# An own order for the last three tiles of a two-layer attention block, with biases added by TensorE there

## The chip, the cores and the metric

The kernel runs on one core of a Trainium2 chip. A core has five engines with queues of their own: PE (TensorE, matrix products into the eight banks of PSUM; PEld is its loading of the stationary operand), DVE (VectorE), ACT (ScalarE), POOL (GpSimd) and SP (SyncE, which here only issues DMAs). Each engine takes its instructions strictly in the order in which the program lists them, and waits at semaphores for the others. The metric is the device time of one execution in microseconds (us), lower is better.

## The reference

2048 tokens (32 sequences of 64) of width 256 pass through a mixture of experts, an attention of 16 heads of 64 with tanh projections, an attention of 16 heads of 16 with a modulated softmax, and a linear layer on values rounded to four bits:

```
moe:   gate = softmax(rms(x) @ wg + cond @ gg); the top two experts of eight, three dense layers each
attn:  q, k, v, out = tanh(... @ W + b);  p = softmax(causal(q k' / 8));  x1 = x + tanh((p v) Wo + bo)
cond2: q, k, v = x1 @ Wqkv' + b;  p = softmax(q k' / 4)
       c   = sigmoid(tanh([x1, cond] @ Wc1' + bc1) @ Wc2' + bc2)          # per token and head
       p   = p * c / (c + 1e-8) scaled by (1 - FI), plus FI * field[key]  # FI = 0.21
       a   = (p v) @ Wout' + bout
ffn:   out = x1 + mxfp4(a) @ mxfp4(W)' + bffn       # blocks of 32 share a power-of-two scale
```

The lines on cond2 are cut down to what is computed for each token; `field` is one vector of 64 shares for each sequence.

## The kernel before

The expert stage runs first (the first 320 us). Then the two attention layers run over TT = 16 tiles of 128 tokens, that is two sequences each. All buffers of that stage lie in `arena`; `ps` is the whole of PSUM.

The order on each engine is written out by hand. PE's loop (`for t in range(2, TT + 4)` at the end of the PE block) mixes four stages of four tiles in one iteration: layer one of tile t (`l1_q`, `l1_k`, `l1_v`, `l1_scores`), its second half for tile t-1 (`l1_turn_p`, `l1_context`, `l1_out`), layer two of tile t-2 (`l1_turn_x1`, `l2_hidden`, `l2_q_or_k`, `l2_coherence`, `l2_scores`, `l2_v`) and of tile t-3 (`l2_turn_p`, `l2_context`, `l2_out`, `l2_turn_q`), and the last product of tile t-4 (`l2_ffn`). ACT's and DVE's loops follow the same pattern. From t = 16 on there is no layer one of a new tile: helpers drop out where their tile does not exist (`exists`), and what is left runs in the same order. PE then executes `tail_busy`: 190 products of constants into an unused bank, whose results nobody reads.

The steps of layer two of one tile, in the order in which one needs the other:

- `l1_out` (L931) on PE, `l1_bias_o` (L1799) on DVE, tanh on ACT (L1281), `l1_residual` (L1808) on DVE gives x1.
- PE turns x1 (L939), ACT copies it into `x1_t` (L1287). From it PE makes the hidden part (L962), q and k (both L947) and v (L981). ACT finishes hidden (L1315), q (L1294) and k (L1304).
- PE computes the coherence (L971) and the scores (L994). DVE takes their maximum (L1844, two halves) and subtracts it (L1850, two halves), ACT takes the exponential (L1330, two halves), DVE sums (L1864) and scales by `r2` (L1865 to L1867, L1872, result `p2`).
- PE turns p2 (L897, two halves), DVE copies it with the field share added (L1881, into `pt2`), PE makes the context (L1015), ACT copies it (L1336), PE makes `a` (L1024), DVE adds the bias (L1888, into `a_rows`).
- DVE rounds to four bits: `block_scales` (L1401 to L1409) and `round_blocks` (L1413 to L1421). PE turns the result (L1032), ACT copies (L1342), PE multiplies (L1041), DVE adds up the output (L1908, `fin`), SP stores it.

Each of these buffers exists once. `l2_x1_bias` (L1816) keeps x1 plus the last bias, and has to wait until L1908 of the tile before has read its buffer; the second half of `l2_turn_p` waits for L1908 of the tile before, since it writes the same bank. A step through `Steps` waits until the instruction before it on DVE is complete.

## Time and profile before

| | us |
|---|---|
| median of 3 runs | 757.79 |
| lowest, highest | 756.41, 757.93 |
| the profiled execution | 760.11 |
| its span, first to last instruction | 758.0 |

In the profiled execution PE is busy for 717.5 us of the span, PEld for 617.0, DVE for 504.8, ACT for 283.2, POOL for 87.4. The whole attention stage lies between about 320 us and the end. A row of a timeline gives the start and the duration of an instruction (or of a run of equal ones), then engine, line and operation; the duration holds the delay until the result is there, and the next instruction can start before it is over.

### The profile page before, as it was taken

The page shows a single profiled execution, that of the slowest core. Times are in us where ns is not written, and L with a number is a line of the kernel's source. Part 1 is how long each engine was busy: PE and PEld are TensorE (multiplying, and loading weights), DVE is VectorE, ACT ScalarE, POOL GpSimd, SP SyncE. Part 2 cuts the span into 40 slices and gives each one's busy share as a digit, 9 for nine tenths or more (in the row PEclk, how much of TensorE's full clock was granted, in tenths as well). Part 3 has the DMA queues.
Part 4 walks back from the last instruction along what each step waited for, and adds up shares of the span by engine and source line. Part 5 has one row for each costly group of instructions (what it writes and reads, how often), then busy time and mean ns, then how long its engine had stood idle before and what let it go on. Part 6 is the DMA issues. An engine that isn't in the chain of part 4 may idle for free.

```text
span 758.0 us, 20462 instructions
## 1 busy us (share of the span) xinstructions
PE 717.5 (95%) x8252; PEld 617.0 (81%) x8252; DVE 504.8 (67%) x1096; ACT 283.2 (37%) x827; POOL 87.4 (12%) x93
## 2 busy tenths in 40 slices
PE   6389999999999999999999999999999999999885
PEld 2279999569999999968888987897888888888774
DVE  3846564744443544244787888789778878887975
ACT  3032221141212112245445545544564555445421
POOL 2131112411212100121101110111011001000000
PEclk9599999999999999999999999999999999999999
DMA  7798111217101103210000010110011000000000
GB/s 285 296 354 313 37 36 58 81 45 257 41 32 43 36 22 112 84 36 22 22 11 22 29 31 2 29 29 23 9 30 30 16 16 29 16 9 9 16 9 15
DMA packets 21257, 49.13 MB, mean 65 GB/s; under 512 B 3179, under 2 KB 14827, under 8 KB 18605
## 3 DMA queue, kind: packets, MB, share of 16 engines
q1 hardware_dynamic: 12112, 32.47, 11.9%
q0 software_dynamic: 3744, 10.49, 4.6%
q10 hardware_dynamic: 5309, 4.87, 1.9%
q8 instruction: 66, 1.08, 0.6%
q14 instruction: 26, 0.21, 0.1%
HBM read 41.00 MB, written 6.82 MB: 63 GB/s over the span
## 4 chain that ended last, share of the span: by engine, by line
PE 87%; DVE 6%; another core or an unknown queue 3%; DMA 1%; ACT 1%; issue 1%; DVEq 0%; SPq 0%; POOL 0%; ACTq 0%; POOLq 0%
PE ps L745 15%; PE ps L846 15%; PE ps L715 8%; PE ps L872 7%; PE ps L779 7%; PE ps L931 7%; PE ps L947 3%; PE ps L897 3%; PE ps L890 2%; PE ps L922 2%; PE ps L1024 2%; PE ps L962 2%; PE ps L981 2%; PE ps L739 1%; PE ps L1041 1%
## 5 line engine op out<-in xcount | busy, mean ns | idle before, releaser
L846 PE MATMUL ps<-arena,l_weights 128*128 128x128 f32 x1024 | 125.9, 277 | 0.5 <-ACT arena L1241 0.5
L745 PE MATMUL ps<-h_t,w_now 128*128 128x128 f32 x1056 | 123.4, 275 | 1.2 <-DVE h_t L1623 1.2
L745 PEld LDWEIGHTS ps<-h_t,w_now 128*128 128x128 f32 x1056 | 120.5, 192 | 1.5 <-issue 1.5
L846 PEld LDWEIGHTS ps<-arena,l_weights 128*128 128x128 f32 x1024 | 119.3, 192 | 2.3 <-ACT arena L1241 1.0
L1166 ACT ACTIVATE h_t<-ps,cols 128x128 f32<-128x128 f32 x132 | 37.6, 367 | 164.1 <-PE ps L715 149.2
L1598 DVE COPY w_now<-arena 128x2048 f32 x33 | 40.5, 1227 | 83.9 <-PE ps L745 76.6
L1247 ACT ACTIVATE arena<-ps,cols 128x128 f32<-128x128 f32 x256 | 74.0, 388 | 46.6 <-PE ps L846 46.6
L610 POOL DMA_INDIRECT arena<-expert_out,slot_of x32 | 33.0, 1032 | 325.5 <-DVE arena L1651 278.6
L715 PEld LDWEIGHTS ps<-xg_t,w_now 128*128 128x128 f32 x528 | 63.4, 192 | 6.6 <-ACT xg_t L1149 4.1
L715 PE MATMUL ps<-xg_t,w_now 128*128 128x128 f32 x528 | 65.0, 276 | 3.6 <-ACT xg_t L1149 3.6
L579 POOL DMA_INDIRECT xg<-in_x,slot_tok x36 | 41.4, 1151 | 188.4 <-PE ps L694 156.4
L779 PE MATMUL ps<-arena,h_t 128*128 x264 | 62.4, 379 | 0.0
L872 PE MATMUL ps<-l_weights,arena 128*64 128x512 f32 x256 | 61.8, 604 | 0.0
L931 PE MATMUL ps<-l_weights,arena 128*128 128x256 f32 x256 | 58.9, 383 | 0.0
L931 PEld LDWEIGHTS ps<-l_weights,arena 128*128 128x128 f32 x256 | 47.4, 190 | 6.0
L779 PEld LDWEIGHTS ps<-arena,h_t 128*128 128x128 f32 x264 | 47.6, 190 | 5.1
L1582 DVE COPY w_now<-arena 128x1024 f32 x33 | 22.9, 694 | 29.3 <-PE ps L715 15.6
L897 PE MATMUL ps<-ident,arena 128*128 128x128 f32 x256 | 38.5, 273 | 1.4 <-DVE arena L1872 1.1
L1623 DVE TENSOR_SCALAR h_t<-ps,cols 128x128 f32<-128x128 f32 x128 | 35.8, 342 | 4.6 <-PE ps L745 4.5
L1767 DVE TENSOR_TENSOR arena<-ps,half_rows 128x512 f32<-128x512 f32 x32 | 21.9, 685 | 24.1 <-PE ps L922 18.6
L872 PEld LDWEIGHTS ps<-l_weights,arena 128*64 128x64 f32 x256 | 15.6, 136 | 22.5 <-issue 21.4
L947 PE MATMUL ps<-arena 128*128 128x128 f32 x256 | 33.7, 275 | 0.0
(303 smaller groups left out, 1077.5 us busy)
## 6 DMA issues: line engine op xcount, KB each, us to landing
arena<-in_experts SPq DMA_DIRECT2D x16, 1024.0 KB, 7.2
expert_out<-y ACTq DMA_DIRECT2D x36, 128.0 KB
arena<-in_x_t SPq DMA_DIRECT2D x2, 1024.0 KB, 6.0
arena<-in_x SPq DMA_DIRECT2D x16, 128.0 KB
out<-arena SPq DMA_DIRECT2D x16, 128.0 KB, 1.7
b<-in_b SPq DMA_DIRECT2D x1, 1024.0 KB, 7.2
l_weights<-in_wq SPq DMA_DIRECT2D x1, 1024.0 KB
l_weights<-in_wk SPq DMA_DIRECT2D x1, 1024.0 KB
```

The costliest lines, as they stand in the source:

```text
L579: pool.indirect_dma_start(out=xg[j % XG][:, :], out_offset=None, in_=t_in["x"], in_offset=bass.IndirectOffsetOnAxis(ap=slot_tok[:, slot_ti ...
L715: last = mm(ps[:, 0, m * P:(m + 1) * P], w1_now[:, k, m * P:(m + 1) * P], xg_t[:, k, :], start=k == 0, stop=k == KH - 1)
L745: last = mm(ps[:, 2, m * P:(m + 1) * P], w2_now[:, k, m * P:(m + 1) * P], h1_t[j % 2][:, k, :], start=k == 0, stop=k == KM - 1)
L779: last = mm(bank(4, HID), h2_t[j % 2][:, k, :], flat[:, bass.ds(at + k * HID, HID)], start=k == 0, stop=k == KM - 1)
L846: last = mm(ps[:, b, c * P:(c + 1) * P], wt[:, k, f:f + P], m_t[:, k, :], start=k == 0, stop=k == KH - 1)
L872: last = mm(ps[r * SEQ:(r + 1) * SEQ, value_bank(t, s), :], m_t[:, k, s * SEQ:(s + 1) * SEQ], wv[:, k, r * 512:(r + 1) * 512], start=k == ...
L897: last = pe.transpose(bank_[:, m * P:(m + 1) * P], p[:, h:h + 2, :], ident[:, :])
L931: last = mm(bank(1, HID), ctx_t[:, c, :], wo[:, c, :], start=c == 0, stop=c == C1 - 1)
L947: last = mm(ps[:, b, c * P:(c + 1) * P], wt[:, k, c * P:(c + 1) * P], x1_t[:, k, :], start=k == 0, stop=k == KH - 1)
L1166: last = f(h1_t[j % 2][:, k, :], ps[:, 0, k * P:(k + 1) * P], ACT.Relu, bias=cols[:, bass.ds(e * KM + at + k, 1)])
L1247: last = f(dst[:, cc, :], ps[:, project_bank(t, n), c * P:(c + 1) * P], ACT.Tanh, bias=col(bias)[:, cc:cc + 1])
L1598: dve.tensor_copy(w2_now[:, :, :].rearrange("p k n -> p (k n)"), arena[:, bass.ds(at, KM * MID)]).then_inc(w2_set, 1)
```

## The change

1. The loops end at t = 15 (PE, ACT) and with `first_part(TT)` (DVE). What is left of tiles p = 13, q = 14, r = 15 is written out as a list on each engine, with PSUM banks chosen by hand (`T1_END` to `FFN_END`). Work of three tiles is mixed there.
2. Layer two has two sets of buffers, chosen by `t % 2`, in the place where the experts' third weights lay. The output has two buffers and two semaphores (`stored`).
3. In these lists PE adds four biases as one more product with a matrix that has ones in its first row only (`first_row`, `first_of_half`), and the field share as a second product with the same stationary operand. DVE or ACT then reads PSUM directly: there is no L1799, no L1888, no L1822, and ACT copies `pt2` and v. POOL adds `x1_bias` for these tiles. Halves of p and of the sums are handed on apart.
4. Layer two in all tiles: `coh` is one operation in place of two, `l2_sums` has one operation less, and the scale by 0.25 in `block_scales` is folded into `act_inv` (two operations more in side stage 8 of the experts).
5. `tail_busy` is gone (190 products); `end_busy(30)` stands before the last tile's last two steps.

```diff
@@ PE
-            def tail_busy(t, last, n): ...
+            def end_out1(t):
+                if t == TT - 1:
+                    pe.wait_ge(pt2_set, 2 * (t - 2) + 1)
+                pe.wait_ge(ctx_set, 2 * t + 2)
+                dst = bank(O_END[t], HID)
+                mm(dst, first_row, row("bo"), start=True, stop=False)
+                for c in range(C1):
+                    last = mm(dst, ctx_t[:, c, :], wo[:, c, :], start=False, stop=c == C1 - 1)
+                last.then_inc(o_ps, 1)
...
+            def end_context2(t):
+                pe.wait_ge(pt2_set, 2 * t + 2)
+                pe.wait_ge(v2_set, 2 * t + 2)
...
+                            mm(dst, values, pt2[t % 2][:, 2 * g + r, q], start=True, stop=False, tile_position=(0, g * PAIR))
+                            last = mm(dst, values, field_t[:, t, q], start=False, stop=True, tile_position=(0, g * PAIR))
+                last.then_inc(out2_ps, 1)
...
-            for t in range(2, TT + 4):
+            for t in range(2, TT):
...
-                tail_busy(t, TT + 2, 20)
...
-                tail_busy(t, TT, 14)
-                tail_busy(t, TT + 1, 20)
...
-                tail_busy(t, TT, 12)
...
-                tail_busy(t, TT, 10)
-                tail_busy(t, TT + 1, 44)
...
-                tail_busy(t, TT + 2, 70)
                 l2_turn_q(t - 3)
-                l1_out(t - 1)
+                if t < TT - 1:
+                    l1_out(t - 1)
+
+            p, q, r = TT - 3, TT - 2, TT - 1
+            pe.wait_ge(first_row_set, 5)
+            end_out1(q)
+            l2_ffn(p - 1)
+            end_turn_p1(r, 0)
+            end_turn_x1(q)
+            end_turn_p1(r, 1)
+            end_q2(q)
+            end_k2(q)
+            end_turn_p2(p, 0)
+            end_context1(r)
+            end_scores2(q)
+            end_turn_p2(p, 1)
+            end_out1(r)
+            end_context2(p)
+            end_turn_x1(r)
+            end_out2(p)
...
+            end_turn_p2(r, 0)
+            end_turn_p2(r, 1)
+            end_ffn(p)
+            end_context2(r)
+            end_out2(r)
+            end_turn_q(q)
+            end_ffn(q)
+            end_busy(30)
+            end_turn_q(r)
+            end_ffn(r)
@@ DVE
             def l2_coherence(t):
...
-                step(ts(coh, ez, 1.0, None, ALU.add))
-                step(dve.reciprocal(coh, coh))
+                step(ts(coh, ez[t % 2], MOD_EPS / (1.0 - FI), (1.0 + MOD_EPS) / (1.0 - FI), ALU.mult, ALU.add))
+
+            def l2_divide():
+                step(tt(r2, coh, z2, ALU.mult))
+                step(dve.reciprocal(r2, r2))
...
+            def end_scales(t):
+                dve.wait_ge(a_ps, t + 1)
+                block_scales(step, bank(OUT2_END[t], HID), q_amax, q_scale, q_inv, None)
+
+            def end_round(t):
+                round_blocks(step, bank(OUT2_END[t], HID), xq[t % 2], q_tmp, q_mag, q_scale, q_inv, act_inv[:, 1:2]).then_inc(xq_set, 1)
...
+            p, q, r = TT - 3, TT - 2, TT - 1
+            first_part(TT)
...
+            end_sum2(q, 0)
+            l1_residual(r)
+            end_sum2(q, 1)
+            end_scales(p)
+            end_round(p)
+            l2_coherence(q)
+            l2_divide()
+            end_share2(q, 0)
+            end_share2(q, 1)
+            l2_max(r, 0)
+            l2_shift(r, 0)
+            l2_max(r, 1)
+            l2_shift(r, 1)
+            l2_coherence(r)
+            end_sum2(r, 0)
+            end_sum2(r, 1)
+            l2_divide()
+            end_share2(r, 0)
+            end_share2(r, 1)
+            end_scales(q)
+            end_round(q)
+            end_result(p)
+            end_scales(r)
+            end_round(r)
+            end_result(q)
+            end_result(r)
@@ POOL
+                if t == 1:
+                    pool.memset(v2[1], 0.0).then_inc(v2_zeroed, 1)
+                    pool.memset(first_row, 0.0).then_inc(first_row_set, 1)
...
+            for t in range(TT - 3, TT):
+                pool.wait_ge(x1_set, t + 1)
+                pool.wait_ge(fin_set, t - 1)
+                pool.wait_ge(x1_bias_set, t)
+                pool.tensor_tensor(x1_bias[t % 2], x1, row("bffn"), ALU.add).then_inc(x1_bias_set, 1)
```

PE in the middle of the end, before: the coherence and `a` of one tile, q and k and the scores of the next, with constant products (L1048) wherever the next step is not ready.

```order
L971 MATMUL ps<-cols,arena 128x16 x2
L1024 MATMUL ps<-arena 128x256 x2
L947 MATMUL ps<-arena 128x128 x8
L1048 MATMUL ps<-before 128x128 x20
L994 MATMUL ps<-arena 64x128 x16
L1048 MATMUL ps<-before 128x128 x44
L981 MATMUL ps<-arena 64x128 x8
L1032 MATMUL ps<-before,arena 128x128 x2
```

The same place now: L1124 turns x1 of tile 15, L1213 is the bias product and L1215 the product with Wout of tile 13, L1149 hidden and L1130 q and k, L1156 and L1159 coherence, L1166 and L1170 v, L1186 the scores of tile 15, and L942 turns p2 of tile 14.

```order
L1124 MATMUL ps<-ident,arena 128x128 x2
L1213 MATMUL ps<-rows,arena 128x256
L1215 MATMUL ps<-arena 128x256 x2
L1149 MATMUL ps<-arena 128x128 x4
L1130 MATMUL ps<-arena 128x128 x8
L1156 MATMUL ps<-rows,arena 128x16
L1159 MATMUL ps<-cols,arena 128x16 x2
```

Real products of another tile stand where the constant ones stood.

DVE in the same stretch, before: the output bias of layer one, the result of one tile, x1 of the next, the two halves with the field share, and then the wait for `a` (L1888) before anything else.

```order
L1799 TENSOR_TENSOR arena<-ps,rows 128x256
L1908 SCALAR_TENSOR_TENSOR arena<-ps,act_inv,arena 128x256
L1816 TENSOR_TENSOR arena<-arena,rows 128x256
L1808 TENSOR_TENSOR arena<-arena 128x256
L1881 TENSOR_TENSOR arena<-ps,arena 128x512 x2
L1888 TENSOR_TENSOR arena<-ps,rows 128x256
L1822 TENSOR_TENSOR arena<-ps,rows 128x16
L1401 TENSOR_REDUCE arena<-arena 128x8
```

DVE now, from the end of the rounding of tile 13 (L1741): coherence (L2179), the divisor (L2182, L2183), the two halves of p2 of tile 14 (L2257), then maximum and shift of tile 15 by halves, its coherence and its sums (L2253).

```order
L1741 TENSOR_TENSOR arena<-arena 128x256
L2179 TENSOR_SCALAR arena<-arena 128x16
L2182 TENSOR_TENSOR arena<-arena 128x16
L2183 RECIPROCAL arena<-arena 128x16
L2257 TENSOR_TENSOR arena<-arena 128x512 x2
L2166 TENSOR_REDUCE arena<-ps 128x8
L2172 TENSOR_TENSOR arena<-ps,arena 128x512
L2166 TENSOR_REDUCE arena<-ps 128x8
L2172 TENSOR_TENSOR arena<-ps,arena 128x512
L2179 TENSOR_SCALAR arena<-arena 128x16
L2253 TENSOR_REDUCE arena<-arena 128x8 x2
```

The operations on x1, on the field share and on the biases have left this stretch, and the next tile's scores follow directly on the p2 of the one before.

## Rows read from the trace of the kernel before

**Rows 1.** The page's first part: busy us, share and instructions of each engine.

```profile
PE 717.5 (95%) x8252; PEld 617.0 (81%) x8252; DVE 504.8 (67%) x1096; ACT 283.2 (37%) x827; POOL 87.4 (12%) x93
```

**Rows 2.** Busy time by stretch: PE, PEld, DVE, ACT, POOL, granted clock, DMA share, GB/s.

```profile
24.00:28.00 4.00, 0.00 (x0) 0.00 (x0) 3.69 (x23) 0.00 (x0) 0.00 (x0) 0.50 0.86 297
...
550.00:600.00 50.00, 50.00 (x721) 42.20 (x719) 40.66 (x87) 26.74 (x78) 4.19 (x4) 1.00 0.08 23
...
708.00:712.00 4.00, 3.11 (x48) 2.75 (x49) 3.90 (x6) 1.56 (x6) 0.00 (x0) 1.00 0.14 39
...
744.00:748.00 4.00, 1.84 (x41) 1.34 (x41) 2.65 (x5) 0.37 (x1) 0.00 (x0) 1.00 0.10 33
```

**Rows 3.** DVE's timeline from 680 us: outputs of five tiles, one wait.

```profile
680.25 0.48 DVE L1908 SCALAR_TENSOR_TENSOR arena<-ps,act_inv,arena 128x256 f32<-128x256 f32 x1 [0.20 <-PE ps L1041]
...
689.68 0.42 DVE L1888 TENSOR_TENSOR arena<-ps,rows 128x256 f32<-128x256 f32 x1 [3.27 <-PE ps L1024]
...
705.93 0.48 DVE L1908 SCALAR_TENSOR_TENSOR arena<-ps,act_inv,arena 128x256 f32<-128x256 f32 x1
...
725.67 0.48 DVE L1908 SCALAR_TENSOR_TENSOR arena<-ps,act_inv,arena 128x256 f32<-128x256 f32 x1
...
744.58 0.48 DVE L1908 SCALAR_TENSOR_TENSOR arena<-ps,act_inv,arena 128x256 f32<-128x256 f32 x1
...
755.45 0.48 DVE L1908 SCALAR_TENSOR_TENSOR arena<-ps,act_inv,arena 128x256 f32<-128x256 f32 x1 [1.68 <-PE ps L1041]
```

**Rows 4.** The chain that ended last: start us, us, what ran.

```profile
701.73 3.51 PE ps L931 x16
...
707.08 0.44 DVE arena L1808
...
709.65 0.94 ACT arena L1315 x4
...
738.47 0.70 DVE arena L1850
...
746.84 0.70 PE ps L1015 x32
747.56 0.38 ACT arena L1336
747.95 0.04 issue
747.99 1.15 PE ps L1024 x4
...
753.83 0.30 PE ps L1032 x2
...
754.58 0.84 PE ps L1041 x6
```

**Rows 5.** DVE's timeline: one tile's rounding, first, a small and last operation.

```profile
749.62 0.42 DVE L1401 TENSOR_REDUCE arena<-arena 128x8 f32<-128x256 f32 x1
...
750.48 0.17 DVE L1406 TENSOR_SCALAR arena<-arena 128x8 f32<-128x8 f32 x1
...
753.35 0.43 DVE L1421 TENSOR_TENSOR arena<-arena 128x256 bf16<-128x256 f32 x1
```

**Rows 6.** ACT's timeline: tanh, four parts of k, two copies of p.

```profile
705.98 0.42 ACT L1281 ACTIVATE arena<-arena 128x256 f32<-128x256 f32 x1 [3.04 <-DVE arena L1799]
...
714.47 1.50 ACT L1304 ACTIVATE arena<-ps,cols 128x128 f32<-128x128 f32 x4 [0.60 <-PE ps L947]
...
716.80 1.08 ACT L1275 COPY arena<-ps 128x512 f32<-128x512 f32 x2
```

**Rows 7.** The one memory fill by POOL at 306 us: duration in ns.

```profile
L615 POOL MEMSET arena<- x1: 524/524/524, 305.9 to 305.9; 128x512 f32 x1
```

**Rows 8.** PE's timeline: turning p, constant products.

```profile
744.60 1.17 PE L897 MATMUL ps<-ident,arena 128*128 128x128 f32 x8 [1.07 <-DVE arena L1872]
...
748.96 4.07 PE L1048 MATMUL ps<-before 128*128 128x128 bf16 x70
```

More of the change, by code:

```diff
@@ L1050, in _, with end_ffn @@
+            def end_ffn(t):
+                pe.wait_ge(xqt_set, t + 1)
+                dst = bank(FFN_END[t], HID)
+                for k in range(KH):
+                    for n in range(PARTS):
+                        last = mm(dst, xq_t[t % 2][:, k, :], wffn[:, k, n, :], start=k + n == 0,
+                                  stop=(k, n) == (KH - 1, PARTS - 1))
+                last.then_inc(f_ps, 1)
             layer1(LAST)
@@ new lines, in end_tanh_o, with end_x1t, end_q2 @@
+            def end_tanh_o(t):
+                act.wait_ge(o_ps, t + 1)
+                act.wait_ge(x1_set, t)
+                f(o_rows, bank(O_END[t], HID), ACT.Tanh).then_inc(o_set, 1)
+            def end_x1t(t):
+                act.wait_ge(x1t_ps, t + 1)
+                act.copy(x1_t[t % 2], bank(X1_END[t], HID).rearrange("p (k q) -> p k q", k=KH)).then_inc(x1t_set, 1)
+            def end_q2(t):
+                act.wait_ge(qk2_ps, 2 * t + 1)
+                for c in range(C2):
+                    last = f(q2_t[t % 2][:, c, :], ps[:, Q2_END[t], c * P:(c + 1) * P], ACT.Identity,
+                             bias=col("bq2")[:, c:c + 1])
+                last.then_inc(qk2_set, 1)
@@ new lines, in end_ez, with end_v2 @@
+            def end_ez(t):
+                act.wait_ge(z_ps, t + 1)
+                f(ez[t % 2], bank(Z_END[t], H2), ACT.Exp, scale=-1.0).then_inc(ez_set, 1)
+            def end_v2(t):
+                act.wait_ge(v2_ps, t + 1)
+                for odd in range(2):
+                    part_ = slice(odd * SEQ, (odd + 1) * SEQ)
+                    act.copy(v2[t % 2][part_, :, odd * D2:(odd + 1) * D2],
+                             ps[part_, V2_END[t], 0:HID].rearrange("p (m d) -> p m d", d=D2)).then_inc(v2_set, 1)
@@ L1366, in _ @@
             l1_exp(1, 1)
-            for t in range(2, TT + 3):
+            for t in range(2, TT):
                 l1_m(t)
@@ L1924, in _, with first_part @@
             l1_residual(0)
-            for t in range(3, TT + 4):
+            def first_part(t):
                 l1_mix(t)
@@ L1944, in _ @@
                 l1_ctx(t - 2, 1)
+            for t in range(3, TT):
+                first_part(t)
                 l2_sums(t - 3)
```

367 lines of the change are left out of this document (310 added, 57 removed).

## The prediction

> **What bounds the kernel now.** I read the busy table first, then the stretches, then DVE's timeline and the chain of waits near the end. PE is busy for 717.5 of 758.0 us [rows 1], and over 550 to 600 us for 50.00 of 50 at the full clock [rows 2]: while four tiles are in the loop, PE sets the time. DVE has slack there; before one of its steps it waits 3.27 us for PE [rows 3]. From the output at 680.25 to that at 705.93 one iteration takes 25.7 us [rows 3].
>
> From about 702 us on there is no new tile, and the picture is another one. The outputs stand at 705.93, 725.67, 744.58 and 755.45 [rows 3]: rounds of 19.7, 18.9 and 10.9 us, though far less work than an iteration's is left. From 708 to 712 DVE is busy 3.90 of 4 us and PE 3.11; from 744 to 748 neither is (2.65 and 1.84) [rows 2]. One of PE's fills alone is 70 products in 4.07 us [rows 8], so even its busy share says too much. The chain of waits goes from PE to DVE to ACT and back in steps of 0.3 to 1.2 us [rows 4]. This is latency: one tile's layer two waits for the buffers and banks of the one before. The last output starts at 755.45 and takes 0.48 us, so the end is at 755.93. The store and what follows to 758.0, and the 2.1 us from there to the profiled 760.11, stay as they are.
>
> **The loop: nothing.** Layer two loses three small DVE operations per tile. The nearest row has 0.17 us, and the next such step starts 0.21 after it [rows 5]; 0.6 us per tile is gone on an engine that waits 3.27 us for PE. PE keeps its order and its work up to t = 15, so the gain is 0. If the waits hid a late DVE it could be up to 0.6 x 13 = 8 us, but with PE at 50.00 of 50 nothing is to be had. In the experts' stage two such operations are added; uncovered they are 0.4 us. POOL's new fills are smaller than, or as large as, the one that takes 0.52 us [rows 7] and stand before a gather for a later tile; I take 0. SP's orders are the same, with one more buffer between result and store: 0.
>
> **The end, added up.** Up to PE's L931 at 701.73 [rows 4] everything stands as before, so I start there. A handover between engines costs 0.03 to 0.04 (the issue piece in [rows 4]); a DVE step costs its duration plus 0.03, or 0.09 less than its duration if nothing depends on it. New PE work: L931 is eight products in 3.51, so 0.44 each [rows 4], and the bias product is a ninth. L1015 takes 0.58 without its start-up (0.70 with it), and twice that, 1.24 with some margin, with the field products. Results come 0.16 after the last issue. `a` becomes three products in place of two: about 1.56 with that delay, where two take 1.15 with their start-up [rows 4].
>
> 1. To the start of tile 15's out product. L931 with bias 4.11, tanh 0.42 [rows 6] and handovers 0.07, x1 0.34, half of p 0.68 and handover 0.04 (an operation on 512 elements has 0.70 [rows 4]), four turns 0.60 (eight have 1.17 from a standing start [rows 8]), handover and first copy 0.52 (two copies have 1.08 [rows 6]), q 0.51, k 1.50 [rows 6] and handover 0.04, scores 0.62, four turns 0.44: 9.9, to 711.6.
> 2. Out product 3.95, context with field 1.40, copy 0.38 and `a` 1.56, handovers 0.11: 7.4, to 718.9. Field additions and bias additions on DVE are not on this path any more.
> 3. Now DVE runs without a gap. Rounding tile 13: the rows of one rounding go from 749.62 to 753.78; less the one small step that is gone, 4.16 - 0.21 = 3.95 [rows 5], of which 3.83 to the next start. Coherence 0.20, divisor 0.50, two half shares 1.18, tile 15's maxima and shifts by halves 2.68 (each about 0.70 [rows 4]), coherence 0.21, half sums 1.26, divisor 0.50, half shares 1.27: 11.6, to 730.6. Meanwhile PE does q, k, hidden, v and scores of both tiles, and ACT its part (L1315 0.94 [rows 4], L1304 1.50 [rows 6]): less than 11.6 on each, so they are hidden.
> 4. Turn, copy, context, copy, `a` of tile 15: 0.64 + 0.63 + 1.44 + 0.41 + 1.60 = 4.7, to 735.3. Rounding tile 14 (3.95) lies beside it.
> 5. Rounding tile 15 3.95, turn 0.30, copy 0.38, last product 0.84, output 0.48 and handovers: 6.0 [rows 4, 5]. The end is at 741.3.
>
> The same adding-up for the old end, with the same rows and handovers, gives 52.7 us from 701.73, where the trace has 54.2: about 3% of small delays is missing. With 3% on 39.6 the end is at 742.4. So 755.93 - 742.4 = 13.5 us go. The profiled 760.11 would be 746.6; the median 757.79 becomes **744.3**.
>
> **What has no row.** The bias products cost between 0.22 (one pass) and 0.5 each, four on the path: -0.9 to +0.3; I take 0.44, as the row has the same shape. The doubled context is the largest doubt: successive products now go to the same columns of the array. At worst they run one after the other. Each of L931's 16 instructions takes 0.22 for 256 columns [rows 4]; a quarter of it, 0.055, for each of 64 instructions is 3.5 us a group. Worked through the list this gives 6.7 us more; none at all hidden is far from L1015's 0.018 each, so I take 1.24 and keep both ends. ACT's copies of v, 0.65 for two (of 0.38 each), have up to 3 us of slack. POOL's addition for 128x256 is bounded by 0.26 (half of the fill [rows 7]) and some 1.5 for two inputs; tile 14's starts at about 707.7 and is needed at 716.2. The fill before the last tile is 30 x 0.058 = 1.75 us [rows 8] in a gap of 2.8.
>
> Rounding now reads `a` from PSUM in two of its operations. The row from PSUM has 0.42 (L1888) [rows 3], the one from SBUF 0.44 (L1808) [rows 4]: no difference. The Trainium skill (Perfetto Trace Analysis, Optimizing Scalar/DVE Operations) gives DVE about 60 ns of access on SBUF and about 125 ns on PSUM. By that the four such reads on the path would add an estimated 0.26 us; the trace does not agree.
>
> **Rivals.** (a) *The doubled context does not overlap.* For it: pairs now share their columns. Against: L1015's and its neighbours' rows. With 3.5 us a group: 751. (b) *POOL's additions hold DVE up.* Each of the last two can begin just as DVE starts on x1 or p. If DVE stands still for the whole addition, at most 2 x 1.5: 747.3. The trace has no POOL work beside DVE at the end, so it says neither. The Trainium skill (SBUF — State Buffer, Who interferes with whom) says that a DVE instruction with two SBUF inputs and a POOL instruction that reads SBUF exclude each other for a whole instruction; by that rule this rival is at hand, but only if they meet. (c) *The lists don't mix the tiles*, because a bank or buffer wait that I read as early comes late; then only the steps taken out count (L1799, L1888, three small steps, part of L1881: 1.4 us in each of three rounds): 753.6. (d) *Slower: the clock.* 190 constant products go and 30 come. From 24 to 28 us, with PE idle, the granted clock is 0.50, that is 1.2 GHz; from 744 to 748 it is 1.00 with PE busy 1.84 of 4 [rows 2]. PE's pieces on the new path are 4.1 + 0.6 + 0.6 + 0.4 + 3.95 + 1.4 + 1.56 + 0.6 + 1.4 + 1.56 + 0.3 + 0.8 = 17.3. If they ran at 1.2 GHz, 17.3 us would be added: 761.6. It turns into a loss once over 13.5 of them run so. Against it: real work fills PE in the new lists, to about 34 of 39.6 us.
>
> **How the numbers follow.** Forecast 0.76, (a) in its full size 0.09, (b) 0.07, (c) 0.04, (d) 0.04. The range takes in the bounds of the bias product below, and (b) and half of (a) above: 741.5 to 749.0. Within 0.2% (1.5 us, about what a measurement can tell from no change) needs two rivals together: 0.01; slower 0.04; faster 0.95.
>
> **What the new profile would show.** Iterations of 25.7 us up to 702 and no waits of PE there. DVE without a gap for about 11 us from near 719 on. Three roundings, with the second right behind tile 15's p2 and the third about 5 us before the end. A context group of 1.2 to 1.4 us; if 2 or more, (a). A granted clock of 1.00 up to the last product; if 0.50 shows, (d). POOL's additions under 1.5 us with no DVE operation stretched; if one is, (b). If DVE waits over 3 us more than once after 711, (c). I am wrong if the last output does not end between 739.5 and 747.

## The result: 13.0 us less

| | before | after |
|---|---|---|
| median, us (4 runs each) | 757.86 | 744.87 |
| lowest, highest | 756.41, 758.33 | 744.04, 746.01 |
| ratio of the runs, 95% interval | | 0.9834 [0.9819, 0.9849] |
| the profiled execution, its span | 760.11, 758.0 | 744.04, 742.3 |
| first projection of the end to the last output ("end stretch") | 701.56 to 755.45: 53.89 | 698.00 to 739.65: 41.65 |

744.3 us had been forecast, 13.5 less than before; 13.0 were measured. The last line of the table is the yardstick of all that follows. It runs from the start of the last product group that both kernels execute in the same place (L931 before, the bias product L1116 ahead of the same projection after) to the start of the last output. It became 12.24 us shorter. PE's timelines, before and after:

```profile
701.56 3.67 PE L931 MATMUL ps<-l_weights,arena 128*128 128x256 f32 x16
```

```profile
698.00 0.65 PE L1116 MATMUL ps<-rows,arena 128*128 128x256 f32 x2
```

The busy time that answers to [rows 1], from the page of the kernel after:

```profile
PE 712.1 (96%) x8218; PEld 612.2 (82%) x8218; DVE 486.7 (66%) x1036; ACT 287.5 (39%) x838; POOL 91.7 (12%) x102
```

PE's busy time fell by 5.4 us, while the span fell by 15.7 (3.56 of them ahead of the end stretch, see the next section): most of what went was waiting. The same stretch of the loop, first of after and then of before (columns as in [rows 2]):

```profile
385.00:697.00 312.00, 312.00 (x4398) 263.52 (x4398) 247.12 (x493) 160.05 (x469) 21.70 (x21) 1.00 0.07 21
```

```profile
385.00:697.00 312.00, 312.00 (x4404) 263.00 (x4404) 254.97 (x528) 161.00 (x472) 20.97 (x20) 1.00 0.07 20
```

DVE has 7.85 us less to do there, in 35 instructions fewer, and PE is busy for 312.00 of 312 us in both. The loop's length can be read as well. It begins at the first product of the attention stage for which PE had to wait, first before and then after:

```profile
325.91 0.44 PE L838 MATMUL ps<-ident,arena 128*128 128x128 f32 x2 [0.88 <-DVE arena L1651]
```

```profile
322.32 0.44 PE L883 MATMUL ps<-ident,arena 128*128 128x128 f32 x2 [0.69 <-DVE arena L1971]
```

From there to the start of the end stretch are 375.65 us before and 375.68 after. The loop gave nothing.

Now the end of the kernel after, as stretches:

```profile
714.00:718.00 4.00, 3.90 (x28) 3.51 (x29) 2.11 (x7) 1.82 (x7) 0.00 (x0) 1.00 0.00 0
718.00:722.00 4.00, 4.00 (x44) 3.29 (x43) 3.69 (x11) 2.74 (x9) 0.00 (x0) 1.00 0.02 4
722.00:726.00 4.00, 3.97 (x119) 3.32 (x117) 2.93 (x6) 2.90 (x9) 0.00 (x0) 1.00 0.01 2
726.00:730.00 4.00, 4.00 (x40) 3.19 (x37) 3.63 (x9) 1.98 (x6) 0.00 (x0) 1.00 0.02 6
```

From 714 to 730 PE is busy for 15.87 of 16 us, with real work only, at a granted clock of 1.00; over 700 to 742 it is 36.85 of 42. Of the end before, [rows 2] showed 3.11 and 1.84 of 4, fills among them. DVE's timeline, the lines on which the reading rests:

```profile
704.38 1.00 DVE L2257 TENSOR_TENSOR arena<-arena 128x512 f32<-128x512 f32 x1
...
706.21 0.69 DVE L2257 TENSOR_TENSOR arena<-arena 128x512 f32<-128x512 f32 x1
...
716.10 0.42 DVE L1723 TENSOR_REDUCE arena<-ps 128x8 f32<-128x256 f32 x1 [1.72 <-PE ps L1215]
...
722.97 0.69 DVE L2166 TENSOR_REDUCE arena<-ps 128x8 f32<-128x512 f32 x1 [1.00 <-PE ps L1186]
...
729.22 0.42 DVE L1723 TENSOR_REDUCE arena<-ps 128x8 f32<-128x256 f32 x1 [0.16 <-PE ps L1215]
...
734.02 0.42 DVE L1723 TENSOR_REDUCE arena<-ps 128x8 f32<-128x256 f32 x1 [0.45 <-PE ps L1215]
...
739.65 0.48 DVE L2270 SCALAR_TENSOR_TENSOR arena<-ps,act_inv,arena 128x256 f32<-128x256 f32 x1 [1.28 <-PE ps L1231]
```

L1723 opens each tile's rounding: 716.10 (tile 13), 729.22 (14), 734.02 (15). Before, the outputs of the last three tiles came in rounds of 19.7, 18.9 and 10.9 us [rows 3], one tile behind the other. Now the third rounding begins 4.8 us after the second. The one gap between 716 and 729 is the 1.00 us ahead of L2166, tile 15's maxima, where DVE waits for PE's scores (L1186). The chain that ended last says who sets the pace (pieces as in [rows 4]):

```profile
698.16 0.49 PE ps L1116 x2
...
704.30 1.80 PE ps L1130 x16
...
706.12 1.51 ACT arena L1594 x4
...
714.42 0.70 PE ps L1213 x2
...
722.24 0.62 PE ps L1186 x32
...
729.18 0.45 PE ps L942 x4
...
729.65 1.08 ACT arena L1619 x2
```

From 714.42 to 729.63 every piece is PE's, but for a handover of 0.03. Up to there PE sets the pace, as it does in the loop. But DVE is close behind: its two shares of tile 15 end at 729.05, and PE turns that tile's p from 729.01 on. How close is measured below.

### The profile page after: what moved, and what is told of

Its sections match the earlier page's. It is cut to its first block, busy times and chain, and to the rows that moved or that the text cites. A ratio compares the mean times of both kernels' runs of the same rounds, so it can differ in the third digit from the quotient of the medians.

```text
span 742.3 us, 20364 instructions
## 1 busy us (share of the span) xinstructions
PE 712.1 (96%) x8218; PEld 612.2 (82%) x8218; DVE 486.7 (66%) x1036; ACT 287.5 (39%) x838; POOL 91.7 (12%) x102
## 4 chain that ended last, share of the span: by engine, by line
PE 93%; DVE 3%; DMA 1%; ACT 1%; issue 1%; POOL 0%; SPq 0%; ACTq 0%; DVEq 0%; POOLq 0%
PE ps L790 16%; PE ps L891 15%; PE ps L760 8%; PE ps L824 8%; PE ps L917 8%; PE ps L976 7%; PE ps L942 4%; PE ps L992 3%; PE ps L935 2%; PE ps L967 2%; PE ps L1007 2%; PE ps L1069 2%; PE ps L1026 2%; PE ps L784 1%; PE ps L1039 1%; PE ps L739 1%
## 5 line engine op out<-in xcount | busy, mean ns | idle before, releaser
L760 PEld LDWEIGHTS ps<-xg_t,w_now 128*128 128x128 f32 x528 | 63.4, 192 | 4.9 <-ACT xg_t L1370 2.4
L760 PE MATMUL ps<-xg_t,w_now 128*128 128x128 f32 x528 | 65.0, 276 | 1.9 <-ACT xg_t L1370 1.9
L976 PE MATMUL ps<-l_weights,arena 128*128 128x256 f32 x224 | 51.5, 383 | 0.0
L976 PEld LDWEIGHTS ps<-l_weights,arena 128*128 128x128 f32 x224 | 41.5, 190 | 5.2
L942 PE MATMUL ps<-ident,arena 128*128 128x128 f32 x256 | 38.3, 273 | 0.1
L1490 ACT ACTIVATE arena<-ps 128x512 f32<-128x512 f32 x32 | 19.0, 605 | 34.6 <-PE ps L935 34.6
```

Source lines behind the costliest of these rows:

```text
L760: last = mm(ps[:, 0, m * P:(m + 1) * P], w1_now[:, k, m * P:(m + 1) * P], xg_t[:, k, :], start=k == 0, stop=k == KH - 1)
L942: last = pe.transpose(bank_[:, m * P:(m + 1) * P], p[:, h:h + 2, :], ident[:, :])
L976: last = mm(bank(1, HID), ctx_t[:, c, :], wo[:, c, :], start=c == 0, stop=c == C1 - 1)
```

## The start of the end stretch moves by itself

The profiled executions differ by 16.07 us, the medians by 13.0. The end stretch accounts for 12.24 of the first; 3.56 lie ahead of it, since it starts at 698.00 instead of 701.56. By the two lines of L838 and L883 above, 3.59 are there already at 325.91 and 322.32, so the difference comes from the expert stage. I ran the kernel after itself once more, beside the version that is told last.

> The kernel after, unchanged, for comparison on the same chip: ratio 0.983 to the kernel before, end stretch 41.6 to 41.7 us whatever the time of its start.

Measured: 747.48 us against 759.70 of the kernel before there, 0.9838 [0.9825, 0.9851]. From its PE and DVE timelines:

```profile
701.89 0.65 PE L1116 MATMUL ps<-rows,arena 128*128 128x256 f32 x2
```

```profile
743.55 0.48 DVE L2270 SCALAR_TENSOR_TENSOR arena<-ps,act_inv,arena 128x256 f32<-128x256 f32 x1 [1.28 <-PE ps L1231]
```

The end stretch is 41.66 us, the same to 0.01, but it begins 3.89 us later than in the other execution of the same kernel, whose time is 3.91 shorter. So where the end stretch begins is not set by the change: it lies between 697.12 and 701.89 in the profiles of the new kernel and its variants, and at 700.02 to 701.56 in the three profiles of the old one. The chip has a part in it, for the median of the kernel before is 756.25 us on one chip and 760.01 on another. The length of the stretch is the kernel's. Below I compare stretches first and times second. Of the 13.0 us between the medians, 12.24 have their place; for the other 0.8 I have none, and the interval of the ratio (11.4 to 13.7 us) holds 12.24 as well.

## Is it the mixing of tiles? One pair un-mixed

In the list of the last three tiles, DVE rounds tile 14 after tile 15's softmax. Here the rounding goes ahead of it, and ACT's list follows (its two exponentials come later):

```diff
+            end_scales(q)
+            end_round(q)
             l2_max(r, 0)
             l2_shift(r, 0)
...
             end_share2(r, 0)
             end_share2(r, 1)
-            end_scales(q)
-            end_round(q)
```

> The changed kernel with one piece of the mixing undone: DVE rounds tile 14 before it takes tile 15's maxima, shifts, sums and shares (and ACT's list is turned round to match). The same instructions. If the mixing of tiles is what wins, DVE waits for turn, copy, context, copy and a of tile 14 (about 4.7 us) with nothing to do, and then has tile 15's part (about 7 us) still before it while PE waits: 6 to 8 us more, 751 to 753. If the gain is in the operations taken out, the time stays at 745.

Measured: 757.97 us, 0.9976 [0.9963, 0.9989] of the kernel before, with an end stretch of 700.19 to 752.98: 52.79, which is 11.14 more than after and 1.1 less than before. Nearly all of the gain is gone, and more than I had written down. PE and then DVE:

```profile
740.81 1.97 PE L942 MATMUL ps<-ident,arena 128*128 128x128 f32 x8 [9.44 <-DVE arena L2257]
```

```profile
731.41 0.42 DVE L1723 TENSOR_REDUCE arena<-ps 128x8 f32<-128x256 f32 x1 [7.25 <-PE ps L1215]
...
740.07 1.29 DVE L2257 TENSOR_TENSOR arena<-arena 128x512 f32<-128x512 f32 x2
```

DVE stands still for 7.25 us while PE works through both tiles' products, since tile 15's softmax now queues behind a rounding whose input is not there; then PE stands still for 9.44 us while DVE does the rounding and the softmax. No instruction was added. Counted from the first projection, PE turns tile 15's p at 40.62 instead of 31.01: 9.61 us later. The other 1.53 are behind that point (12.17 to the last output instead of 10.64), where the turning takes 1.97 us instead of 1.04:

```profile
738.00:742.00 4.00, 1.19 (x6) 1.19 (x7) 3.19 (x8) 0.66 (x2) 0.00 (x0) 0.50 0.00 0
```

The granted clock is 0.50, that is 1.2 GHz, after PE has done nothing from 734 to 738. To tell order and clock apart, the same kernel was given work for PE in that wait, 130 products of an identity into an unused bank:

```diff
+            for _ in range(130):
+                mm(bank(2, P), ident_h[:, :], ident_h[:, :], start=True, stop=True)
             end_turn_p2(r, 0)
```

> As e4_unmix_tile14, with 130 products of an identity (0.061 us each, 8.0 us) on TensorE in the wait of 9.44 us in which its clock fell to 0.50. If e4's 11.1 us were latency of an un-mixed pair plus a clock that fell: the products of 740.8 to 744 (1.97 and 1.49 us at the low clock, 1.04 and 0.82 at the high one) give 1.6 us back, end stretch 51.0 to 51.5 us against 52.79. If the clock had no part in it: 52.8.

Measured: 757.82 us, 0.9971 [0.9957, 0.9985], end stretch 700.26 to 751.70: 51.44, inside what was expected. PE's timeline and the stretch:

```profile
731.28 7.42 PE L1324 MATMUL ps<-before 128*128 128x128 bf16 x130
...
740.89 1.26 PE L942 MATMUL ps<-ident,arena 128*128 128x128 f32 x8 [2.19 <-DVE arena L2259]
```

```profile
738.00:742.00 4.00, 1.81 (x22) 1.44 (x20) 3.27 (x8) 1.04 (x2) 0.00 (x0) 1.00 0.00 0
```

The turning still starts 40.63 us after the first projection, and from there to the last output it is 10.81, near the 10.64 of after. So of the 11.14 us, 9.6 belong to the order and 1.35 to the clock. By time the two kernels can't be told apart (their intervals cover each other); by the stretch they can.

The filled version keeps everything else that the change brought: the second buffers, the biases and the field share on PE, the removed steps, and the rest of the order. All of that together is worth 53.89 - 51.44 = 2.45 us without this one piece of the order. Parts 2 and 3 of the change were not run alone; the mixed order needs the second buffers, so their shares can't be told apart by these runs.

## Is it the operations that were taken out?

Part 4 of the change alone, put into the kernel before:

```diff
-                step(ts(coh, ez, 1.0, None, ALU.add))
-                step(dve.reciprocal(coh, coh))
+                step(ts(coh, ez, MOD_EPS / (1.0 - FI), (1.0 + MOD_EPS) / (1.0 - FI), ALU.mult, ALU.add))
...
-                step(stt(r2, coh, MOD_EPS, z2, ALU.add, ALU.mult))
+                step(tt(r2, coh, z2, ALU.mult))
                 step(dve.reciprocal(r2, r2))
-                step(stt(r2, coh, 1.0 - FI, r2, ALU.mult, ALU.mult))
```

(and the scale by 0.25 folded into `act_inv`)

> The kernel before with part 4 of the change alone: three small DVE operations fewer per tile in layer two, two more in the experts' stage. My theory: PE sets the time up to 702 us, so nothing is won there; in the end each of three rounds of DVE's chain loses 0.7 us and the last rounding 0.2, so the stretch from the start of L931 near 702 us to the last output shrinks from 54.2 to about 52 us, and the time is 755.6 (1.9 to 2.5 us less than before). Rival, that DVE's small operations set the pace of every tile: 0.7 us in each of 16 tiles, 11 us less, 747.

Measured: 758.5 us against 760.01, 0.9986 [0.9972, 1.0001]. The end stretch is 700.78 to 753.93, that is 53.15: 0.74 us less. Four of its DVE lines:

```profile
724.56 0.48 DVE L1906 SCALAR_TENSOR_TENSOR arena<-ps,act_inv,arena 128x256 f32<-128x256 f32 x1 [0.22 <-PE ps L1041]
...
726.06 0.42 DVE L1808 TENSOR_TENSOR arena<-arena 128x256 f32<-128x256 f32 x1 [0.48 <-DVE arena L1816]
...
731.23 0.42 DVE L1886 TENSOR_TENSOR arena<-ps,rows 128x256 f32<-128x256 f32 x1 [3.55 <-PE ps L1024]
...
732.96 0.18 DVE L1857 TENSOR_SCALAR arena<-arena 128x16 f32<-128x16 f32 x1 [0.20 <-ACT arena L1323]
```

The expectation missed, for the gain is a third of it, and its rival of 11 us is out. By time the run can't be told from no change. The three steps that went are worth 0.71 us in each of the first two rounds (by the distance to the next start 0.21, 0.29 and 0.21), and 0.21 in the last rounding. The rounds shrink by 0.33, 0.20 and 0.21 us. The rest is in waits that the kernel before has short or not at all: 0.20 for ACT's L1323 in both rounds, 0.22 for PE's L1041 in the first, 0.48 at L1808 in the second, for which the profile names only DVE's own L1816. Behind the shorter steps DVE meets other waits sooner, and they take about half of the gain. The wait at L1886 is 3.55 us in both kernels.

## What bounds the middle of the end? Four edits

I had forecast that DVE runs there without a gap and hides PE's work. The trace has PE without a pause, and DVE with one gap of 1.00 us, in which it waits for PE. Three edits take from PE or move its work, one moves POOL's. Their expectations count from 42.0 us, which is the length to the end of the last output; what is won or lost is compared with them.

**The bias product of v left out** in the last tiles (its output lacks that bias):

```diff
-                    for odd in range(2):
-                        part_ = slice(odd * SEQ, (odd + 1) * SEQ)
-                        mm(ps[part_, V2_END[t], s * P:(s + 1) * P], first_of_half[part_, :], half_row("bv2")[part_, :],
-                           start=True, stop=False, tile_position=(odd * SEQ, odd * SEQ))
```

> The changed kernel with the bias of v left out in the last three tiles (PE's L1166, two groups of 0.37 us in each of tiles 14 and 15); the output lacks that bias. In the profile of the changed kernel PE has no pause from 714.4 to 729.2 us. If PE bounds that stretch, both groups are won: the stretch from L1116 near 698 us to the last output goes from 42.0 to about 40.5 us, 743.4. If DVE bounds it, as I predicted, at most DVE's pause of 1.0 us before L2166 shrinks by 0.7 and the rest is hidden: 41.3 or more.

Measured: 743.61 us against 756.25, 0.9827 [0.9807, 0.9847]; end stretch 698.96 to 739.39, that is 40.43: 1.22 us less. DVE's timeline:

```profile
723.04 0.69 DVE L2162 TENSOR_REDUCE arena<-ps 128x8 f32<-128x512 f32 x1
```

The wait of 1.00 us before tile 15's maxima is gone. Work of PE alone was taken away, and 1.22 us were won. That is more than the 0.7 that a bound by DVE would have allowed and less than the 1.5 of a bound by PE alone. For one tile's v PE now needs 1.02 us instead of 1.92 in the chain, so 0.90 each went from tile 14 (ahead of tile 15's scores) and tile 15 (behind them). The first is won in full: the maxima start 24.08 us after the first projection instead of 24.97. Of the second 0.34 are won at the third rounding. PE's timeline says why:

```profile
728.58 1.26 PE L942 MATMUL ps<-ident,arena 128*128 128x128 f32 x8 [0.20 <-DVE arena L2253]
```

PE now waits 0.20 us for DVE's share of tile 15, and from 723.04 to there DVE has no gap. So PE bounds this part of the kernel after, but with about 1 us less of PE's work ahead of the scores DVE bounds it.

**The field product left out** (the output lacks the field share):

```diff
-                            mm(dst, values, pt2[t % 2][:, 2 * g + r, q], start=True, stop=False, tile_position=(0, g * PAIR))
-                            last = mm(dst, values, field_t[:, t, q], start=False, stop=True, tile_position=(0, g * PAIR))
+                            last = mm(dst, values, pt2[t % 2][:, 2 * g + r, q], start=True, stop=True, tile_position=(0, g * PAIR))
```

> The changed kernel with the field product left out of the last three contexts (32 of 64 instructions in each group); the output lacks the field share there. The group then takes about 0.65 us as in the kernel before and not 1.1. If PE bounds the end, all three are won, 3 x 0.5: from 42.0 to about 40.5. If DVE bounds the middle, only tiles 13 and 15 are on the path: about 41.0. Had the doubled context been serial (my rival a), a group would have had 3.5 us, and 5 us or more would be won.

Measured: 743.65 us, 0.9828 [0.9806, 0.985]; end stretch 697.12 to 737.92, that is 40.80: 0.85 us less for 96 products in three tiles. DVE's timeline:

```profile
721.68 0.69 DVE L2165 TENSOR_REDUCE arena<-ps 128x8 f32<-128x512 f32 x1 [1.00 <-PE ps L1186]
```

Here the gap stays at 1.00, since what was taken away lies before 714 (tile 13's context) and behind 724. From the first projection, the roundings begin at 17.70, 30.57 and 34.83 instead of 18.10, 31.22 and 36.02: 0.40, 0.25 and 0.54 us from one tile's context each. On PE a group takes 0.65 us with 32 instructions and 1.17 with 64, so the doubled context costs PE 0.52 each; the first two are not won in full, because PE then waits 0.41 us for DVE's x1 of tile 15, and because DVE goes from tile 15's maxima to the second rounding without a gap. The expectation was 1.5 us if PE bounds the end and 1.0 if only tiles 13 and 15 count. At the third rounding 1.19 us are won, at the last output 0.85, so the run is nearer to the second. The 0.34 between them are lost, and the section on e9 below shows to what.

**Scores of tile 15 ahead of the v of tile 14**, to end DVE's gap without leaving anything out:

```diff
-            end_v2(q)
             end_hidden(r)
             end_scores2(r)
+            end_v2(q)
```

(and the same in ACT's list)

> The changed kernel with PE's v of tile 14 behind the scores of tile 15 (and ACT's copy of v behind its tanh). If DVE bounds the middle of the end, its pause of 1.0 us before tile 15's maxima goes and the time falls by up to 1.0 us. If PE bounds it, nothing is won: PE has the same work before it can turn p of tile 15, and context 14 has to wait for ACT's later copy of v: 0 to 0.8 us more (42.0 to 42.8 from L1116 to the last output).

Measured: 745.67 us, 0.9858 [0.9834, 0.9883]; end stretch 698.87 to 741.39, that is 42.52: 0.87 us more. PE and DVE:

```profile
721.79 0.70 PE L1186 MATMUL ps<-arena 32*64 32x128 f32 x32 [0.68 <-ACT arena L1594]
```

```profile
730.96 0.42 DVE L1723 TENSOR_REDUCE arena<-ps 128x8 f32<-128x256 f32 x1 [0.72 <-PE ps L1215]
```

The gap ahead of the maxima is indeed gone, but PE now waits 0.68 us, for ACT's k, where it had had v to do, and 0.23 more ahead of tile 14's context, for ACT's copy. The sum is near the 0.87 that were lost, at the edge of the 0 to 0.8 that had been expected of a bound by PE. PE's lost time comes back as a wait of DVE further on. Filling DVE's gap at PE's cost makes it slower.

**POOL's addition for tile 14 later**, so that it no longer runs beside DVE's share of p:

```diff
                 pool.wait_ge(x1_bias_set, t)
+                if t == TT - 2:
+                    pool.wait_ge(s2_ps, t + 1)
                 pool.tensor_tensor(x1_bias[t % 2], x1, row("bffn"), ALU.add).then_inc(x1_bias_set, 1)
```

> The changed kernel with POOL's addition for tile 14 held until the scores of tile 14 are there, when DVE takes a maximum from PSUM. In the changed kernel this addition (0.73 us from 704.11) meets DVE's share of p (L2257, two inputs in SBUF), which has 1.00 us there and 0.69 elsewhere. If POOL and DVE exclude each other, that share has 0.69 again; since ACT's k is on the chain there, the time changes by less than 0.3 us. If the long share has another cause, it stays at 1.00.

Measured: 744.48 us, 0.9833 [0.9811, 0.9856]; end stretch 698.66 to 740.32, that is 41.66: no difference. First POOL's addition in the kernel after, then DVE and POOL in this one:

```profile
704.11 0.73 POOL L660 TENSOR_TENSOR arena<-arena,rows 128x256 f32<-128x256 f32 x1 [25.18 <-DVE arena L2231]
```

```profile
705.05 0.69 DVE L2259 TENSOR_TENSOR arena<-arena 128x512 f32<-128x512 f32 x1
...
708.34 0.69 DVE L2250 COPY arena<-ps 128x512 f32<-128x512 f32 x1 [1.10 <-PE ps L1109]
```

```profile
709.28 0.73 POOL L662 TENSOR_TENSOR arena<-arena,rows 128x256 f32<-128x256 f32 x1 [29.69 <-PE ps L1188]
```

With the addition out of the way the share takes 0.69 us instead of 1.00. DVE then waits 1.10 us for PE where it had waited 0.78: the 0.32 us were covered. The stretching is real, and it was off the path.

## The fills

The kernel before without its 190 constant products, and the kernel after without its 30:

```diff
-                tail_busy(t, TT + 2, 20)
...
-                tail_busy(t, TT + 2, 70)
```

(all six calls)

> The kernel before without its 190 constant products. If these held the clock up (the mechanism of my slower rival), the granted clock falls to 0.50 somewhere after 702 us and PE's pieces there become twice as long: 760 to 770. If they only fill idle time, the granted clock stays at 1.00 up to the last product and the time is that of before within 1 us.

```diff
-            end_busy(30)
```

> The changed kernel without its 30 constant products. If the last fill matters, the last turn and product (0.30 and 0.84 us) take twice as long or more, some 1 to 1.5 us: 746. If not: 744.9 within 1 us and granted clock 1.00 up to the last product.

Measured: before without fills 761.57 us, 1.0022 [1.0006, 1.0038], end stretch 55.12 (1.23 more); the kernel after without fills 747.08 us, 0.9833 [0.9809, 0.9856], end stretch 42.29 (0.64 more). First the kernel before without fills, then PE and DVE of the kernel after without them:

```profile
734.00:738.00 4.00, 0.49 (x32) 0.24 (x20) 3.83 (x8) 0.36 (x1) 0.00 (x0) 0.59 0.00 0
738.00:742.00 4.00, 3.28 (x23) 2.44 (x24) 3.10 (x8) 1.24 (x3) 0.00 (x0) 0.50 0.00 0
```

```profile
740.76 1.46 PE L1231 MATMUL ps<-wffn,arena 128*128 128x256 bf16 x6 [0.47 <-ACT arena L1627]
```

```profile
742.26 0.48 DVE L2269 SCALAR_TENSOR_TENSOR arena<-ps,act_inv,arena 128x256 f32<-128x256 f32 x1 [1.91 <-PE ps L1231]
```

Without fills PE does 0.49 of 4 us from 734 to 738, and the clock is 0.50 behind that. The first two rounds keep their 19.7 and 18.9 us; the loss is in the last. In the new end the granted clock stays at 1.00 without any fill up to 740, and only the last product meets the low one, after a wait of 2.64 us at L1223: it takes 1.46 us instead of 0.83. The wait for it grows from 1.28 to 1.91 us and nothing else moves. Both runs lie between their two expectations: the clock does fall to 0.50, and it costs 1.2 and 0.6 us. In the new lists no more than 0.6 us was left for constant products to win.

## A version with products ahead of waits

PE being the bound, two groups of products were put ahead of a wait whose result they don't need: the bias product of `a` before the wait for the context's copy, and, for tile 15, the context products with the field share before the wait for the turned p.

```diff
             def end_context2(t):
+                if t == TT - 1:
+                    pe.wait_ge(v2_set, 2 * t + 2)
+                    for part_ in range(2):
+                        if part_:
+                            pe.wait_ge(pt2_set, 2 * t + 2)
...
+                                    last = mm(dst, values, pt2[t % 2][:, 2 * g + r, q] if part_ else field_t[:, t, q],
+                                              start=part_ + s + r == 0, stop=part_ == 1 and s + r == 2, tile_position=(0, g * PAIR))
...
-                pe.wait_ge(out2_set, t + 1)
                 dst = bank(OUT2_END[t], HID)
                 mm(dst, first_row, row("bout"), start=True, stop=False)
+                pe.wait_ge(out2_set, t + 1)
```

> The kernel after with two products of the end put ahead of a wait: the bias product of each second output projection before the wait for the context's copy, and, for tile 15 alone, the eight context products that use the field share before the wait for the turned probabilities. If TensorE bounds the end from tile 15's turning on, and in the last tile the copy by ScalarE (the projection of tile 15 waits 0.47 us for it in the profile of the kernel after), each bias product of 0.44 us lies in a wait: end stretch (start of the first output projection to start of the last output) 40.5 to 41.2 us against 41.65, ratio 0.001 lower than the kernel after on the same chip. If the end were bound by VectorE there: 41.6, no change.

Measured: 746.1 us (746.01 to 746.93), where the kernel after has 747.48 (746.4 to 747.95) and the kernel before 759.7 on the same chip: 0.9827 [0.9813, 0.984]. The end stretch is 700.52 to 741.61, that is 41.09, 0.57 us less than after; the expectation had wanted 0.45 to 1.15, so it is met near its lower end. From its DVE timeline:

```profile
718.26 0.42 DVE L1738 TENSOR_REDUCE arena<-ps 128x8 f32<-128x256 f32 x1 [1.35 <-PE ps L1230]
...
731.38 0.42 DVE L1738 TENSOR_REDUCE arena<-ps 128x8 f32<-128x256 f32 x1 [0.16 <-PE ps L1230]
```

The wait ahead of the first rounding is 1.35 us instead of 1.72, and the one ahead of the third (0.45 in the kernel after) is gone. From the first projection the third rounding begins at 35.12 instead of 36.02. So 0.90 us are won there, but only 0.57 at the last output. Behind the second rounding DVE now runs into the third without a wait, so the rest of the chain is DVE's. The missing 0.33 us, as the 0.34 of the run without the field product, is in the third rounding itself. DVE's second step of it, and POOL's addition for that tile:

```profile
736.09 0.52 DVE L1739 TENSOR_SCALAR arena<-arena 128x8 f32<-128x8 f32 x1
```

```profile
735.86 0.72 POOL L660 TENSOR_TENSOR arena<-arena,rows 128x256 f32<-128x256 f32 x1 [28.50 <-DVE arena L2285]
```

A step on eight values for each partition takes 0.52 us instead of 0.17 [rows 5] while POOL adds, and the next begins that much later. In the kernel after the addition has ended (733.70 and 0.72 us, that is 734.42) just before that step at 734.48. Rival (b) had come true after all, in a kernel that reaches the place earlier. The stretch explains 0.57 us of the 1.38 between the medians; the rest may be chance, since the two intervals against the kernel before overlap.

### The last addition put behind the rounding

```diff
                 pool.wait_ge(x1_bias_set, t)
+                if t == TT - 1:
+                    pool.wait_ge(xq_set, TT)
                 pool.tensor_tensor(x1_bias[t % 2], x1, row("bffn"), ALU.add).then_inc(x1_bias_set, 1)
```

> As e9_hoist, and POOL's addition for tile 15 waits until that tile's rounding is done. In e9_hoist it ran from 735.86 for 0.72 us beside DVE's second step of the third rounding, which took 0.52 us instead of 0.17. If POOL held DVE up there, that step is back at 0.17 and the end stretch is 0.35 shorter: 40.7 us against 41.09, 0.9 less than after, ratio about 0.982. If DVE's long step had another cause, 0.52 stays and the stretch is 41.1. If POOL's addition, which would now start about 0.1 us behind the rounding, comes too late for the last output, the wait before the output grows above 1.28 us.

Measured: 746.85 us against 758.35 on its own chip, 0.9846 [0.9832, 0.986], though the end stretch is 699.25 to 739.99, that is 40.74. In DVE's timeline the step is back at 0.17:

```profile
734.82 0.17 DVE L1741 TENSOR_SCALAR arena<-arena 128x8 f32<-128x8 f32 x1
...
739.99 0.48 DVE L2287 SCALAR_TENSOR_TENSOR arena<-ps,act_inv,arena 128x256 f32<-128x256 f32 x1 [1.28 <-PE ps L1248]
```

The stretch is what was expected, and the time is not: 0.982 lies outside the interval, and the ratio is no better than that of the kernel after. The span ends at 745.6, which is 5.6 us behind the start of the last output; in the kernel after it is 2.65 (742.3), in e9 2.7. The end of the program has instructions of its own (they all carry the line number L167). POOL's among them, first here and then in the kernel after (count, duration in ns, start):

```profile
L167 POOLq DRAIN  x1: 6883/6883/6883, 738.5 to 738.5; - x1
```

```profile
L167 POOLq DRAIN  x1: 6883/6883/6883, 733.7 to 733.7; - x1
```

POOL's drain takes 6.88 us and starts with its last addition. In the kernel after it is over at 740.6, before the last store is (SP's own last wait ends near 742.1), and costs nothing. Here it ends at 745.4, and all engines leave at 745.5. In the profiles the 0.35 us won inside became some 2.6 lost in all: from the first projection to the end of the span e12 has 46.3 us, e9 43.8 and the kernel after 44.3. By time the interval of e12 overlaps with that of e9, so the loss is read from the spans. By the span e9, without this wait, is the shortest kernel here that computes everything. The way to have both would be an addition ahead of the rounding, into a third buffer; it wasn't tried.

## Why the prediction was right, and where it was not

**The loop, 0.** Right: PE at 312.00 of 312 us with 7.85 us less of DVE's work.

**The end.** The sum gave 39.6 us from L931 to the end of the last output, 40.7 with the 3%; the trace has 698.16 to 740.13, that is 42.0. By its steps:

| step | forecast | measured | |
|---|---|---|---|
| 1, to tile 15's projection | 9.9 | 10.8 | 698.16 to 708.96 |
| 2, to tile 13's `a` | 7.4 | 7.1 | to 716.10 |
| 3, to tile 14's `a` and tile 15's p | 11.6 | 13.1 | to 729.22 |
| 4, to tile 15's `a` | 4.7 | 4.8 | to 734.02 |
| 5, to the end | 6.0 | 6.1 | to 740.13 |

*Step 3* is the one that failed in its reasoning, not only in its size (11.6 forecast, 13.1 measured). It said that DVE would run without a gap and that PE's work was "less than 11.6 on each, so they are hidden". DVE's own terms were good: from 716.10 to the end of tile 13's shares at 721.96 and from 722.97 to the end of tile 15's at 729.05 it works for 11.9 us. What the sum left out is that its second half needs tile 15's scores, and PE gets to them only after everything that the list puts before them, at 722.17. The comparison of totals hid that. So the 13.1 are 11.9 of DVE's work, the 1.00 of that wait, and 0.16 for PE's `a` of tile 14. Runs e5 and e7 show how far the claim was off: PE's work ahead of the scores counts in full (0.89 of 0.90 us in e5), and of its work behind them 0.34 of 0.90 (e5) and 0.25 of 0.52 (e7) counted, the rest being hidden as forecast. PE was also busier than the 34 of 39.6 us that I had put down: 36.85 of 42.

*Step 1* was short by a term. From PE's turns of tile 14's p to ACT's k the sum had a first copy of p and q (0.52 + 0.51). In the chain PE's instructions of q and k follow there, all sixteen, for 1.80 us, and ACT's L1594 starts behind them at 706.12.

(The prediction's 718.9 behind step 2 should be 719.0, which is what its later times go by.)

The 3% of small delays, 1.1 us, covered about half of these two misses. That the time still came out 0.6 us from the forecast is partly luck: the medians' difference is 0.8 larger than the stretch's, and the gain of 13.5 us that was forecast for the end stands against 12.24 in the stretch.

**The bias products.** Taken at 0.44 each; the pieces of L1116 in the chain have 0.49 and 0.44. **The doubled context**: taken at 1.24 us a group. The pieces for tile 13 go from 712.85 to 714.00, which is 1.15; rival (a) with 3.5 us more a group is refuted. **POOL's addition**: bounded by 0.26 and 1.5, measured 0.73.

**Rivals.** (b) has its mechanism and not its price: one DVE operation was stretched by 0.31 us, outside the chain. In e7 and e9, where the last addition meets the third rounding, it costs 0.34 us on the path. The Trainium skill (SBUF — State Buffer, "Who interferes with whom") says that DVE with two inputs in SBUF contends with a GpSimd instruction that reads SBUF; the row at 704.38 with its two inputs in `arena` agrees, and the same operation without POOL beside it has 0.69. The two records overlap for 0.46 us there, and the operation grew by 0.31. The same section lists `tensor_scalar` among the operations that can take the shared ports; the 0.52 instead of 0.17 us in e9 fits that. (c) is refuted: no DVE wait over 1.72 us after 711, and e1 shows that the small steps alone are worth 0.74. (d) is refuted in size: with the 30 constant products the clock stays at 1.00 up to the last product, and without any fill only that product is slow and 0.64 us are lost, not 17.3. e4 shows when it would have counted: with PE idle through a wait of 9.44 us it costs 1.35.

**PSUM as DVE's source.** The rounding's first step reads PSUM in 0.42 us, as long as from SBUF before [rows 5]. The row decided rightly against the added access time.

## What to carry to other kernels

Where the last tiles of a pipeline run one behind the other, look for the order of the lists before looking for operations to remove: one swap in DVE's list moved 9.6 us, while taking out small operations moved 0.7. When such a list is added up, follow each engine's queue up to the very product that the other engine needs next; comparing totals per stage (11.6 against "less than 11.6") does not show who is late. After the change PE is the bound of the middle, so the next gain is products placed ahead of waits, not work given over to PE. It is a small one: with some 1 us less of PE's work DVE sets the pace (e5, e7). And the last instruction of POOL wants to be early: what is behind it counts from there.

## What was not expected of the hardware

POOL's drain at the end of the program takes 6.88 to 6.89 us in the traces of the new kernel and its variants, from the start of POOL's last addition on. In the kernel before, where POOL ends with gathers, it takes 8.74 us from 631.4 on, and costs nothing. A POOL instruction of 0.72 us that runs 1.5 us before the last output (e12) made the span behind that output 5.6 us long instead of 2.7. Two profiled executions of the same kernel reach the same instruction 3.9 us apart (698.00 and 701.89), with a length behind it that agrees to 0.01 us. In those two, 1.92 us of it are there at the product of L760 that starts at 38.97 and 40.89, ahead of which PE waits 0.52 and 2.14 us for the tokens that ACT copies, and all of it by PE's L883 (322.32 and 326.21); the cause of the longer wait was not traced. And beside a POOL addition of 0.73 us a DVE operation with two inputs on 512 elements grew from 0.69 to 1.00 us, one on eight elements from 0.17 to 0.52.
